# Scaling, halves and transpose of the quantised FFN input moved ahead of the last piece of h's FP4

## The reference

```python
def fp4_quant_dequant(x):
    xb = x.reshape(shape[:-1] + (shape[-1] // BLOCK, BLOCK))
    scale = jnp.maximum(jnp.max(jnp.abs(xb), axis=-1, keepdims=True) / 6.0, 1e-12)
    xn = xb / scale
    idx = jnp.searchsorted(_MID, jnp.abs(xn))
    return (_GRID[idx] * jnp.sign(xn) * scale).reshape(shape)
gate = fp4_linear(x, w_gate); y = fp4_linear(x, w_up)      # 512 -> 1408
h = jax.nn.silu(gate) * y
return fp4_linear(h, w_down)                               # 1408 -> 512
```

## Time and profile before

| | |
|---|---|
| median of the runs | 1887.38 us |
| the profiled execution | 1892.68 us, span 1891.0 us |
| TensorE busy | 1783.6 us (94%), 11513 matmuls, 11513 weight loads |
| VectorE, ScalarE, GpSimd busy | 1566.1, 1415.8, 1191.7 us |
| TensorE idle before L485, until xqT's transpose landed | 15.0 us |
| TensorE idle before L613, until an hqT transpose landed | 12.2 us |
| instruction packets on DMA queue q8 | 93, 1.52 MB |
| mean granted TensorE clock | 0.971 |

### The profile page before, as it was taken

One profiled execution on the slowest core, in us unless ns is written; L12 is line 12 of the kernel. 1 busy time (PEld: TensorE's weight loads), 2 busy tenths in 40 slices (PEclk: granted clock), 3 DMA queues, 4 the chain that ended last, 5 costly groups with the idle time before them and its releaser, 6 DMA issues. The chain is left out here.

```text
span 1891.0 us, 36967 instructions
## 1 busy us (share of the span) xinstructions
PE 1783.6 (94%) x11513; PEld 1046.0 (55%) x11513; DVE 1566.1 (83%) x3213; ACT 1415.8 (75%) x2943; POOL 1191.7 (63%) x1189
## 2 busy tenths in 40 slices
PE   4557999999999999999999999999999999999996
PEld 3434556556555565555556555655565555555553
DVE  8987888888887888879888888888888888889993
ACT  7765777787877777777777877777787877776753
POOL 7765666566666656666666666656666665656652
PEclk8668999999999999999999999999999999999998
DMA  6334454344444534444444454444443454445332
GB/s 214 101 75 94 120 115 111 108 120 124 108 114 114 127 99 116 120 111 116 113 121 109 121 115 116 109 110 119 123 110 108 122 126 101 115 104 110 88 66 62
DMA packets 342116, 211.47 MB, mean 112 GB/s; under 512 B 275200, under 2 KB 281856, under 8 KB 341920
## 3 DMA queue, kind: packets, MB, share of 16 engines
q1 hardware_dynamic: 341920, 209.10, 44.1%
HBM read 125.93 MB, written 17.30 MB: 76 GB/s over the span
## 5 line engine op out<-in xcount | busy, mean ns | idle before, releaser
L485 PE MATMUL bank<-wgTh,xqT 128*128 128x512 f16 (+1 forms) x1536 | 556.9, 363 | 15.0 <-DMA xqT<-xqs 15.0
L485 PE MATMUL bank<-wuTh,xqT 128*128 128x512 f16 (+1 forms) x1536 | 556.6, 362 | 0.0
L1077 POOL TENSOR_TENSOR stage<-stage,hs 128x512 f32<-128x512 f32 (+1 forms) x192 | 190.4, 992 | 433.9 <-DVE stage L1286 433.9
L613 PE MATMUL bank<-wdTh,work 128*128 128x512 f16 x704 | 269.0, 382 | 12.3 <-DMA work<-stage 12.2
L485 PE MATMUL bank<-wgTl,xqT 128*128 128x512 f16 (+1 forms) x768 | 278.4, 362 | 0.0
L485 PE MATMUL bank<-wuTl,xqT 128*128 128x512 f16 (+1 forms) x768 | 278.1, 362 | 0.0
L614 PE MATMUL bank<-wdTl,work 128*128 128x512 f16 x704 | 267.7, 380 | 0.0
L615 PE MATMUL bank<-wdTh,work 128*128 128x512 f16 x704 | 267.4, 380 | 0.0
L485 PEld LDWEIGHTS bank<-wgTh,xqT 128*128 128x128 f16 x1536 | 157.1, 102 | 160.0 <-DMA xqT<-xqs 22.7
L1130 POOL TENSOR_TENSOR stage<-stage,hinv 128x512 f32<-128x512 f32 (+1 forms) x192 | 238.9, 1246 | 8.2 <-DVE hinv L1371 8.1
L485 PEld LDWEIGHTS bank<-wuTh,xqT 128*128 128x128 f16 x1536 | 163.8, 107 | 131.8 <-issue 1.1
(11 more groups left out here) (209 smaller groups left out, 3954.4 us busy)
## 6 DMA issues: line engine op xcount, KB each, us to landing
mb<-max_dram SPq DMA_DIRECT2D x64, 512.0 KB, 4.0
x<-in_x_dram SPq DMA_DIRECT2D x64, 256.0 KB, 2.9
cf<-in_ctx_dram SPq DMA_DIRECT2D x64, 256.0 KB, 3.7
cn<-in_ctx_dram SPq DMA_DIRECT2D x64, 256.0 KB, 3.8
wb<-warp_dram SPq DMA_DIRECT2D x128, 128.0 KB, 3.4
out_dram<-ob SPq DMA_DIRECT2D x64, 256.0 KB, 3.7
xb<-in_x_dram SPq DMA_DIRECT2D x60, 256.0 KB, 2.6
work<-stage SPq DMA_TRANSPOSE x192, 3.1
```

The costliest lines, as they stand in the source:

```text
L485: i = e.matmul(o[:, 0:width], x, w[:, c, n0:n0 + width], start=first and k < 2, stop=last and k >= 4)
L613: e.matmul(DOWN[:, :], hi, wdT[0][:, c0 + c, :], start=(c0 + c == 0), stop=False)
L1077: e.tensor_tensor(blocks(hx[:, n0:n0 + w]), blocks(hx[:, n0:n0 + w]), per_block(hs2[:, n0 // BLOCK:(n0 + w) // BLOCK]), ALU.mult).then_inc ...
```

## The change

In the loop's turns, `pool_x_qs` of t7 stands ahead of `pool_h_qs` 2 of t9 instead of behind it. `act_x_hi` of t7 stands right behind `act_silu` 2, ahead of `act_uc`, `act_h_hi` 2, `act_Sbd` and `act_sq`. `dve_x_lo` of t7 stands right behind `dve_ham` 2, ahead of `dve_nr_neg` and `dve_h_lo` 2. `sp_xqT` is called for t7 at the end of the turn, between `sp_mb_in` and `sp_hqT` 2, instead of for t8 at the start of the next turn; tile 2's call goes to the end of the prologue. TensorE's order is the same.

```diff
@@ sp_turn
-            t8 = Tile(u - 8)
+            t7 = Tile(u - 7)
-            if t8.live(NT):
-                sp_xqT(e, t8)
             if t6.live(NT):
                 sp_wb_in(e, t6)
...
             if t5.live(NT):
                 sp_mb_in(e, t5)
+            if t7.live(NT):
+                sp_xqT(e, t7)
             if t9.live(NT):
                 sp_hqT(e, t9, 2)
@@ sp_start
-... sp_hqT(e, T[0], 2); sp_mb_in(e, T[4])
+... sp_hqT(e, T[0], 2); sp_mb_in(e, T[4]); sp_xqT(e, T[2])
@@ act_turn
                 act_silu(e, t8, 2)
+            if t7.live(NT):
+                act_x_hi(e, t7)
             if t6.live(NT):
                 act_uc(e, t6, 0)
...
                 act_sq(e, t6)
-            if t7.live(NT):
-                act_x_hi(e, t7)
@@ pool_turn
-            if t9.live(NT):
-                pool_h_qs(e, t9, 2)
             if t7.live(NT):
                 pool_x_qs(e, t7)
+            if t9.live(NT):
+                pool_h_qs(e, t9, 2)
@@ dve_turn
                 dve_ham(e, t8, 2)
+            if t7.live(NT):
+                dve_x_lo(e, t7)
             if t6.live(NT):
                 dve_nr_neg(e, t6)
...
                 dve_ve(e, t6)
-            if t7.live(NT):
-                dve_x_lo(e, t7)
```

More of the change, by code:

```diff
@@ L442, in sp_start @@
             sp_w_T(e, 8); sp_w_T(e, 9); sp_w_T(e, 10); sp_x1_in(e, T[3]); sp_xqT(e, T[1]); sp_cn_in(e, T[3]); sp_hqT(e, T[0], 0); sp_x_in(e, T[9])
-            sp_hqT(e, T[0], 1); sp_rows_out(e, T[7]); sp_hqT(e, T[0], 2); sp_mb_in(e, T[4])
+            sp_hqT(e, T[0], 1); sp_rows_out(e, T[7]); sp_hqT(e, T[0], 2); sp_mb_in(e, T[4]); sp_xqT(e, T[2])
         @block.sync
@@ L1215, in pool_turn @@
                 pool_vk(e, t6)
+            if t7.live(NT):
+                pool_x_qs(e, t7)
             if t9.live(NT):
                 pool_h_qs(e, t9, 2)
-            if t7.live(NT):
-                pool_x_qs(e, t7)
             if t6.live(NT):
```

## The result

The changed kernel takes 1940.08 us (median of 4 runs, 1937.42 to 1943.11), beside it the kernel before 1887.66 (4 runs, 1887.36 to 1894.13): a ratio of 1.0265, 95% interval 1.0243 to 1.0288, 52.4 us slower. The forecast was slower, 1916 us, in a range of 1884 to 1948. The sign holds, and so does the mechanism in the usual turns; the loss is nearly twice the one worked out.

The account below looks back on a forecast made before the run. TensorE, busy 94% of the span, was taken as the bound. The terms -12.2 + 7.6 + 21.7 + 6 + 5 gave +28.1 us, so 1916 us; own range 1900 to 1932, stated range 1884 to 1948.

Parts of the forecast that it names:

- rival A: In plain turns un gets the port ahead of x_lo, so xqT and hqT 2 go late: 1946 us, chance 0.22.
- What goes, -12.2: TensorE's waits for xqT in 14 turns of the loop vanish, xqT being issued about 2.3 us earlier: 12.2 us gained.
- Plain turns, +7.6: In 40 plain turns h_lo 2 ends 1.14 us later, so down 2 starts 0.19 late: 7.6 us lost.
- Gate turns, +21.7: In 14 gate turns h_q 2 waits for x_qs and hqT 2 for xqT's issue: 1.55 us each, 21.7 lost.
- New collisions, +11: Instruction packets of q8 now meet hqT 2: 6 us in four gate turns, 5 in about nine plain ones.
- Prologue and drain, 0: Prologue and drain, where VectorE or the h chain set the end, stay unchanged within 1 us.
- B (faster): VectorE's new order costs less than the slack and hqT 2 is never late: 12.2 us gained, 1875 us, chance 0.15.
- C (a draw): No port wait counts, only order and SyncE's issue: -1.8 us, 1886 us, chance 0.15.

Follow-up runs that it names:

- the two plain-turn experiments: The change kept out of gate turns, against the kernel before: with the new order in the drain 1906.47 us, with the drain's old order 1895.01 us.

## Why the prediction was right in sign and short in size

**Where the number fell.** 1940 us lies outside the forecast's own range, 1900 to 1932. It lies in the stated one because that takes in rival A, and rival A's port race was lost in 3 of 40 plain turns of the loop, not in all, and in three turns of the drain. Most of the rest of the way is half clock (12.1 us in the loop, 4.8 in the drain), which neither the sum nor a rival has. To that extent the range held by luck.

**What goes, -12.2.** Right in kind: L485 has left the list of waits, 10.2 us in the loop and some 2 in the drain.

**Plain turns, +7.6.** Measured 3.4. x_lo came first to the port by 0.03 us (0.02 forecast), xqT was issued 20.02 us into the turn (20.02 forecast), hqT 2 was 1.03 later (1.14 forecast). With a slack of 0.96, 0.1 us less delay leaves half of the 0.19. Rival A fell in 37 of these 40 turns; it happened in three, and in the drain.

**Gate turns, +21.7.** Measured 23.1, 1.65 us a turn against 1.55. The middle of two bounds was taken, and M does count: M and x_qs start 0.02 us apart, x_qs takes 1.29 instead of 1.06, and h_q 2 ends 1.73 us after M's start instead of 0.91, which is 0.82 later. By the Trainium skill's rule ("SBUF — State Buffer", Who interferes with whom) M, with its two inputs in SBUF, would hold off x_qs for its whole 0.46; the trace has x_qs 0.23 longer, so the rule's direction holds and its size is half here. The forecast saw one wait where two are: qk for St, 0.80 us (the single swap on GpSimd makes it alone), then down 2 for hqT 2. The total is near since both spend the same delay: hqT 2 is 1.98 later, and less 0.42 of slack and with 0.05 to the start that is 1.61.

**New collisions, +11.** The term that failed: measured 27.7. Seven gate turns are over 30.63 by 0.5 us or more, 16.5 us in all, where 4 x 1.5 = 6 was forecast, and the plain ones give 11.0 instead of 5. That hqT 2 would be hit was right: it lands after 3.8 to 5.2 us where it is met, 2.7 otherwise. So was the count for q8: four gate turns, whose longer idle time is 6.5 us, against 6. What the step left out is, first, the clock: with the long waits the granted clock falls to 0.5 for a while, and this costs 12.1 us of busy time. Where no half clock is granted, a like amount of busy time is gone: 9.6 us in the swap on SyncE, 12.2 with qk twice. The waits alone are 15.6 us. They hold, second, 2.2 us of longer idle time in the two gate turns that q14 packets hit; I had looked for no other stream than TensorE's. Third, 5.6 us are longer idle time of the three plain turns in which un won the port, two of which packets met as well.

**Prologue and drain, 0.** Failed for the drain: +11.3 in the trace, 12.5 between the two plain-turn experiments. I had looked at what bounds the end of the drain, and not at its first five turns, in three of which un came to the port first. Those turns have the same four steps with less work around them; that this is what turns the race is likely and not shown.

**Rivals.** B (faster) falls with L613's 25.8 us. C (a draw) falls with 1.34 us for h_q 2. Of the two profiled executions, 1920.8 forecast and 1943.1 measured, the 22.3 us between are: collisions with their clock +16.7, drain +11.3, the loop's waits +2.0 (10.2 gone, not 12.2), gate turns +1.4, plain turns -4.2, prologue -4.9. Still open is why un wins the port in three plain turns of the loop, and whose instructions the q14 packets carry.

## What to carry to other kernels

A step that is moved ahead to remove a wait spends the slack of everything that it passes, on each queue: here 10 us of waits were bought with 0.82 us on VectorE's port and 1.3 us of SyncE's issue time in turns whose next steps, St as well as hqT 2, had less than that. Work out the slack for each kind of turn, the drain's too, and for every consumer behind the moved step, not only for the last; then try the change in one kind of turn at a time, which costs a few conditions once and one line for each further kind. Where a port race delayed a short instruction, moving the long one on the idler engine (un behind sch, 3.9 us) gave more here than moving the late transpose's last step (x_lo, nothing).

## What was not expected of the hardware

How late a packet comes decides whether it delays a DMA transpose. In the twelve traces of this case all 143 transposes after 215 us that a q8 packet meets 0.6 to 2.3 us after their issue, with no q14 packet in their time, land late, after 3.4 to 5.3 us instead of 2.7 (384 columns) or 3.0 (512). Of 298 that one meets after 2.3 to 2.95 us, 91 are late; of 299 after 2.95 to 4.9 us, none. An issue that is moved a little can so gain or lose 1.9 us: in the kernel before, xqT landed after 4.96 us with the packet 2.38 us behind its issue, and after 3.07 with it at 2.46. The q14 packets do the same in less measure: of the 15 transposes that one alone meets after 1.5 to 2.1 us, 14 land after 3.4 to 4.1 us, and 83 of the 85 late transposes without a q8 packet have one in their time. The q8 packets keep their place in TensorE's stream, one in 248 instructions on average: half of the 93 come within 6 instructions of the same place before and after the change, the farthest is 52 off.

Between 215 and 1900 us of the changed kernel the granted clock fell to 1.2 GHz nine times, each time with a wait of TensorE of 1.95 to 3.18 us in it or just before it, for 3.41 or 6.83 us. In three of the nine it fell during the wait, in six 0.4 to 1.3 us after TensorE had gone back to work. In the turn from 243.91 a wait of 2.38 us thus cost 2.7 us more.

A 128x8 instruction on VectorE is held up by the port like a large one: nr_neg takes 0.16 us alone, 0.72 behind un before, and 1.15 after.
